# The last batch's attention tail in an order and banks of its own, filler rows issued by ScalarE, two steps of each batch moved by one q unit

## The chip, the cores and the metric
The kernel runs on one core of a Trainium2 chip. The metric is device time in microseconds (us) from start to end of one launch. Engines by short name: PE is TensorE (matmuls; PEld its weight loads), DVE is VectorE, ACT is ScalarE, POOL is GpSimd, SP the sync engine that issues most DMAs. SBUF is on-chip memory, PSUM holds the results of matmuls in eight banks of 128 partitions x 2 KB.

## The reference, cut to what matters
8 batches of 512 tokens, width 256, all in float32:

```python
h = conv31_depthwise(embed_table[x]) + conv_b
n = layernorm(h)
q, k, v = split(n @ w_qkv)                    # 16 heads of 64
q = softmax(q * 64**-0.5, over the 64 columns of a head)
k = softmax(k, over the 512 tokens)
h = h + ((k^T q per head) applied to v) @ w_out + b_out
n = layernorm(h)
p = sigmoid(n @ router_w.T); the two best of 8 experts, weights normalised
h = h + sum over those two: w * (relu(n @ W1[e])**2) @ W2[e]   # widths 4 x 256, 4 x 512
```

Since q is not mixed over tokens, each batch folds context, v and w_out into one 256 x 256 matrix m, so that the attention's output is n @ m.

## The kernel before
**Stages.** First the convolution, to about 93 us. Then `attend` works through the 8 batches, to about 487 us. Then `experts` goes through 71 tiles of 128 queue rows, each with the weights of one expert, to the end.

**How a batch of `attend` is cut.** Products in full float32 precision of the large ones are made from three float32r products (high x high, high x low, low x high: `split_product`), so most operands exist as a pair `_hi`, `_lo`: ACT copies the high part out of PSUM, DVE subtracts it to get the low part. For batch b: `xt` turns the normalised rows; `xt_high` and `xt_low` make their pair; eight `q_unit` (6 matmuls of 512 columns each) give q; for each, DVE takes the maximum and subtracts it (`q_shift`), ACT takes the exponential (`q_exps`), DVE sums (`q_total`), POOL normalises (`q_norm`). Eight `k_unit` give k turned, with `k_max` on DVE and `k_exp` on ACT, `k_turn` on PE (4 transposes into bank 3 or 4) and `k_take` on ACT out of it. `k_turn(b, c)` waits until `k_take` of c - 2 has emptied the bank.

**The tail of a batch** (12 uses of banks 5, 6, 7 in turn, `tail_bank`): `context_of` 0 and 1 (k^T q; DVE's `context_take` scales it), `g_of` 0 and 1 (context x w_out; ACT's `g_take` 0 to 3 empty the four banks), `m_of` (16 products in true float32), `m_high` and `m_low`, `attention_of` (24 products), `add_attention` and `ln2_stats` on DVE, `root2` on POOL (the reciprocal root), `ln2_apply` (the normalised rows, written to the tile `row`), `x2_turn`, `x2_take`, `router`, `logits_take`, `router_turn`, `prob_exp`, then on DVE `route_best` (the two best experts; ends in `counted`), `ranks` on PE (how many tokens go to each expert before this one) and `route_slots` on DVE (the queue slot of each row; ends in `slot`), last `enqueue` on POOL: 8 indirect DMAs of 128 rows of 258 floats each to `queue_d` in HBM.

**The order is written out by hand.** Every engine has a function `step(b, prev, nxt, old)`, called once per batch, in which the tail of `prev` and the routing of `old` are laced between the q and k work of b. `steps` calls it for n = -1 to 9, so the last two calls (b is None) hold only the tail of batch 7 and the routing of batches 6 and 7. In those calls stand also `w1_high` and `w1_low` (the expert weights w1 are split in high and low, in two pieces kk of 3072 columns) and `w1_pads` (POOL zeroes the padding). On SP, the last piece of w2 (`raw_in[3]`, 1536 KB) is loaded when `w1_low(0)` is done, after the store of batch 7's rows.

**Between the stages.** The engines' queues are in order. After `slot` of batch 7, DVE works out the table of tiles (`table.end_i`, `ends_ready`; at last `table.ready`). SP waits for `ends_ready` and writes one filler block of 128 rows after each of the 8 experts' queues: a register load (L764) and a DMA (L765) each. Then it waits until all fillers have landed (`table.filled`), reads the first 8 tile addresses into registers (`row_at`, L1546), waits for all enqueued rows (`queued`) and loads 8 tiles (L1551). ACT and DVE split w2 (`w2_high(2)`, `w2_high(3)`, `w2_low(2)`, `w2_low(3)`) before the first tile's `x_high` and `x_low`.

Of the kernel before, what the change touches and what calls it, by code (L numbers as in the profile page):

```python
# [20 lines left out]
F32 = mybir.dt.float32  # L21
# [90 lines left out]


class Dispatch:
# [3 lines left out]
    def __init__(self, sbuf, sem):  # L118
# [14 lines left out]
            "table_consts", "filler_ready", "ends_ready", "filled", "table_chain", "table_ready"))  # L133

# [27 lines left out]
def tower(nc, x, embeddings, conv_w, conv_b, w_qkv, w_out, b_out, router_w, w1, w2, out):  # L162
    top = ExitStack()
    with top:
# [35 lines left out]
        with ExitStack() as attn_ctx:  # L200
# [8 lines left out]
            with ExitStack() as ctx:  # L209
                attending = attend(nc, ctx, sem, bank, ident, base, base0, rw_t, w1, w2, h_d, store, h_in, loaded, h_stored, raw_in,  # L210
                       table, queue_d, out, second_half, wqk_hi, wqk_lo, wv_t, wo, bo_all,
                       w1_parts, w1_hi_ready, w1_lo_ready, w1_zero)
        with ExitStack() as ctx:
            expert_work = experts(nc, ctx, sem, bank, ident, store, raw_in, table, queue_d, out, w1_parts, w1_lo_ready,
                                  w1_zero, attending.queued, attending.stored)
# [401 lines left out]
def attend(nc, ctx, sem, bank, ident, base, base0, rw_t, w1, w2, h_d, store, h_in, loaded, h_stored, raw_in,  # L617
           table, queue_d, out, second_half, wqk_hi, wqk_lo, wv_t, wo, bo_all,
           w1_parts, w1_hi_ready, w1_lo_ready, w1_zero):
    def sbuf(name, shape, dt=F32):  # L620
# [49 lines left out]

    stored = [sem(f"stored{i}") for i in range(2)]
# [6 lines left out]
        sem(n) for n in ("q_shifted", "q_exp_ready", "q_inv_ready", "q_ready", "k_max_ready"))  # L678
    k_exp_ready, k_psum, k_ready, tail_chain, tail_psum = (
# [23 lines left out]

    def steps(engine, step):
# [10 lines left out]
        for n in range(-1, BATCHES + 2):  # L715
            step(at(n), at(n - 1), at(n + 1), at(n - 2))

    def sync(sp):
# [38 lines left out]
        steps(sp, step)  # L757

        sp.wait_ge(w1_lo_ready, 1)
        sp.dma_start(raw_place(store, 3), raw_piece((w1, w2), 3)).then_inc(raw_in[3], 16)  # L760

        sp.wait_ge(table.ends_ready, 1)
        for e in range(EXPERTS):
            at = sp.value_load(table.end_i[0:1, e:e + 1], min_val=0, max_val=FILLER_ROW)  # L764
            sp.dma_start(queue_d[bass.ds(at, P), :], table.filler[:]).then_inc(table.filled, 16)  # L765
    def gpsimd(pool):
# [68 lines left out]
        def enqueue(b):  # L835
            wait_apart(pool, slots_ready, b.nth(1, 1), pool_passed)
            for c in range(TOPK):
                for t in range(TT):
                    pool.indirect_dma_start(  # L839
                        out=queue_d, in_=row[:, t, c, :], in_offset=None,  # L840
# [14 lines left out]
        def step(b, prev, nxt, old):  # L855
            enqueue(old)
            if b is None:
                w1_pads(prev)
# [12 lines left out]
        steps(pool, step)  # L871

    def scalar(act):
# [63 lines left out]
        def step(b, prev, nxt, old):  # L937
# [12 lines left out]
            if b is None:  # L950

                w1_high(prev, 0)
                w1_high(prev, 1)
# [833 lines left out]
```

## Time and profile before

| | |
|---|---|
| median of 3 runs | 737.45 us (732.85 to 738.35) |
| the profiled execution | 736.28 us, its span 734.6 us |
| busy share of the span | PE 86%, PEld 75%, DVE 64%, ACT 42%, POOL 44% |
| batches 0 to 7 (93 to 450 us) | PE busy 340.31 of 357 us |
| last tail to first expert tile (450 to 510 us) | PE busy 21.11 of 60 us |
| experts (510 to 734 us) | PE busy 198.72 of 224 us |

Times in rows of the trace are us from the start of the span. In a timeline row: start, length, engine, line, operation, output <- inputs, how many; in brackets the idle time of the engine before it and what ended it. L877 is a helper's line for all copies of ACT, L1311 that of all split products of `attend`. A PE row's length holds the time for the last result to come out; so the next product can start before it ends. SPq and ACTq are DMA issues on those engines.

### The profile page before, as it was taken

Reading aid. Unit: us, or ns where it says so; the run is one execution under the profiler, and the core shown is the slowest. Engines: PE = TensorE matmul, PEld = TensorE weight load, DVE = VectorE, ACT = ScalarE, POOL = GpSimd, SP = SyncE. Lnnn points to the kernel's source line nnn. Section 1 sums busy time; section 2 is a strip of 40 time slices with the busy share of each in tenths; the row PEclk is TensorE's granted clock in tenths of the full one; section 3 lists DMA queues with packets and bytes.
Section 4 is the critical chain, followed back from the end, with each engine's and each line's share of the span. In section 5 each row is a group of like instructions: output and inputs, shape, how many; then the busy total and the mean of one; then the engine's idle time right before and its main releaser. Section 6 shows DMA issues by size and latency. Waiting matters only on the chain.

```text
span 734.6 us, 15772 instructions
## 1 busy us (share of the span) xinstructions
PE 632.1 (86%) x5032; PEld 547.8 (75%) x5032; DVE 469.7 (64%) x1216; ACT 306.8 (42%) x668; POOL 322.0 (44%) x292
## 2 busy tenths in 40 slices
PE   6997579999999999999999997523999999988881
PEld 6897457787877878778778785512899999987871
DVE  6475585777779777797787963573554554555540
ACT  3460135343353443533435335330544544555541
POOL 6350250330814608237073260635254454466574
PEclk9999689999999999999999999855999999999996
DMA  6551990010111101112010010423355445466663
GB/s 227 191 105 23 207 341 11 2 57 3 58 58 52 66 1 60 57 45 73 2 59 30 31 57 2 143 95 108 52 83 81 75 82 81 76 112 111 106 97 45
DMA packets 37216, 58.12 MB, mean 79 GB/s; under 512 B 5726, under 2 KB 31066, under 8 KB 36506
## 3 DMA queue, kind: packets, MB, share of 16 engines
q1 hardware_dynamic: 22434, 36.14, 16.9%
q0 software_dynamic: 14160, 20.13, 15.3%
q8 instruction: 61, 1.00, 0.6%
q10 hardware_dynamic: 520, 0.51, 0.2%
q14 instruction: 41, 0.34, 0.2%
HBM read 28.30 MB, written 27.42 MB: 76 GB/s over the span
## 4 chain that ended last, share of the span: by engine, by line
PE 65%; DVE 11%; DMA 7%; issue 5%; ACT 5%; POOL 3%; SPq 3%; DVEq 0%; POOLq 0%; ACTq 0%
PE bank L1311 20%; PE bank L1703 16%; PE bank L1383 8%; DMA out<-y,token_at 5%; PE bank L1354 4%; PE bank L1371 2%; PE bank L1719 2%; PE bank L521 2%; PE bank L522 2%; DVE xn L1009 2%; PE bank L542 2%; PE bank L1340 2%; POOL out L1583 2%; ACT k_exps L895 2%; DVE row L1089 1%
## 5 line engine op out<-in xcount | busy, mean ns | idle before, releaser
L1583 POOL DMA_INDIRECT out<-y,token_at x71 | 111.6, 1572 | 109.7 <-SPq L1563 107.6
L839 POOL DMA_INDIRECT queue_d<-row,slot x64 | 68.8, 1075 | 165.8 <-DVE slot L1148 148.7
L1660 DVE SCALAR_TENSOR_TENSOR act_w<-relu,queue_rows 128x512 f32<-128x512 f32 (+1 forms) x71 | 44.6, 629 | 102.5 <-ACT relu L1606 52.3
L1311 PE MATMUL bank<-xt_hi,w_first 128*128 128x512 f32 x256 | 95.1, 417 | 0.9 <-DVE second_half L1026 0.9
L1311 PE MATMUL bank<-w_first,xt_hi 128*128 128x512 f32 x256 | 83.8, 409 | 2.2 <-DVE xt_lo L1016 1.5
L831 POOL TENSOR_TENSOR second_half<-second_half,q_inv 128x512 f32<-128x512 f32 x64 | 64.9, 1041 | 44.0 <-DVE q_inv L1035 43.8
L887 ACT ACTIVATE second_half<-second_half 128x512 f32<-128x512 f32 x64 | 39.6, 632 | 87.9 <-DVE second_half L1026 87.9
L895 ACT ACTIVATE k_exps<-bank,k_negmax 128x512 f32<-128x512 f32 x64 | 44.1, 690 | 75.3 <-DVE k_negmax L1042 75.1
L1703 PE MATMUL bank<-w_hi,a_hi 128*128 x214 | 66.0, 308 | 1.6 <-DVE a_lo L1666 1.1
L1703 PE MATMUL bank<-w_lo,a_hi 128*128 x214 | 59.9, 280 | 0.1
L1606 ACT ACTIVATE relu<-bank 128x512 f32<-128x512 f32 (+1 forms) x71 | 35.4, 498 | 58.7 <-PE bank L1703 57.9
L1703 PE MATMUL bank<-w_hi,a_lo 128*128 x214 | 59.6, 278 | 0.0
L1311 PEld LDWEIGHTS bank<-w_first,xt_hi 128*128 128x128 f32 x256 | 46.9, 192 | 15.6 <-issue 2.7
L1383 PE MATMUL bank<-g,wv_t 128*128 128x256 f32 x256 | 56.7, 380 | 1.2 <-ACT g L877 1.2
L1311 PEld LDWEIGHTS bank<-xt_hi,w_first 128*128 128x128 f32 x256 | 49.2, 192 | 11.3 <-DVE second_half L1026 1.8
L1023 DVE TENSOR_REDUCE q_max<-bank 128x8 f32<-128x512 f32 x64 | 42.1, 657 | 22.6 <-PE bank L1311 22.6
L1383 PEld LDWEIGHTS bank<-g,wv_t 128*128 128x128 f32 x256 | 48.6, 190 | 8.4 <-ACT g L877 1.6
L1042 DVE TENSOR_REDUCE k_negmax<-bank 128x1 f32<-128x512 f32 x64 | 42.8, 680 | 13.4 <-PE bank L1311 13.1
L1311 PE MATMUL bank<-w_first,xt_lo 128*128 128x512 f32 x128 | 50.9, 398 | 0.0
L1311 PE MATMUL bank<-xt_lo,w_first 128*128 128x512 f32 x128 | 50.8, 397 | 0.0
L1703 PE MATMUL bank<-w_first,x_hi 128*128 x142 | 40.1, 364 | 9.7 <-DVE x_lo L1648 6.5
L1693 PE MATMUL bank<-ident,queue_rows 128*128 128x128 f32 x142 | 27.7, 279 | 23.3 <-DMA queue_rows<-queue_d 23.3
(183 smaller groups left out, 1564.3 us busy)
## 6 DMA issues: line engine op xcount, KB each, us to landing
queue_rows<-queue_d SPq DMA_DIRECT2D x71, 129.0 KB, 2.3
store<-in_L_ffn_w SPq DMA_DIRECT2D x4, 1536.0 KB, 9.2
out<-res SPq DMA_DIRECT2D x8, 512.0 KB, 2.9
h_d<-store SPq DMA_DIRECT2D x6, 512.0 KB, 9.0
h_in<-h_d SPq DMA_DIRECT2D x6, 512.0 KB, 4.0
windows<-taps_d SPq DMA_DIRECT2D x4, 512.0 KB, 5.8
wqk<-in_L_attn_w_qkv SPq DMA_DIRECT2D x1, 2048.0 KB, 13.9
out<-y,token_at POOLq DMA_INDIRECT x71, 4.0
```

What stands on the lines that cost most here:

```text
L831: nc.gpsimd.tensor_tensor(v, v, q_inv[:, b.par, u].unsqueeze(2).to_broadcast([P, 8, DH]), ALU.mult).then_inc(q_ready, 1)
L839: pool.indirect_dma_start(out=queue_d, in_=row[:, t, c, :], in_offset=None, out_offset=bass.IndirectOffsetOnAxis(ap=slot[:, TT * c + t:TT ...
L887: nc.scalar.activation(v, v, ACT.Exp, scale=SCALE).then_inc(q_exp_ready, 1)
L895: nc.scalar.activation(k_exps[:, c % 2], qk_bank(10 + c)[:], ACT.Exp, bias=k_negmax[:, c:c + 1], accum_out=k_sum[:, b.par, c:c + 1]).then_ ...
L1023: link(nc.vector.tensor_reduce(q_max[:, u % 2], src, AX, ALU.max), q_chain, b, Q_LINKS, 2 * u + 1 - (u > 0))
L1042: nc.vector.tensor_reduce(k_negmax[:, c:c + 1], qk_bank(10 + c)[:], AX, ALU.max, negate=True).then_inc(k_max_ready, 1)
L1311: last = nc.tensor.matmul(o, a, c, start=(n == 1), stop=(n == 3 * len(pairs)))
L1383: last = nc.tensor.matmul(tail_bank(6)[:, DIM * kk:DIM * kk + DIM], wv_t[:, a, P * kk:P * kk + P], g[:, a], start=(a == 0), stop=(a == PAI ...
L1583: pool.indirect_dma_start(out=out, in_=y[:, j % RING, :], in_offset=None, compute_op=ALU.add, out_offset=bass.IndirectOffsetOnAxis(ap=toke ...
L1606: nc.scalar.activation(relu[:, u % 2, 0:width], bank[2 + u % 2][:, 0:width], ACT.Relu).then_inc(relu_ready, 1)
L1660: nc.vector.scalar_tensor_tensor(out=act_w[:, u % 2, 0:width], in0=relu[:, u % 2, 0:width], scalar=rows[:, u, DIM:DIM + 1], in1=relu[:, u ...
L1703: last = nc.tensor.matmul(o, a, c, start=(n == 1), stop=(n == parts))
```

## The change
1. In each batch, `k_turn(b, 7)` on PE goes from the end of the batch to behind `q_unit(b + 1, 0)`; `g_of(prev, 1)` goes behind `q_unit(b, 5)`; ACT takes `q_exps(b, 3)` between `g_take` 1 and 2.
2. The last two calls of `step` are replaced by an order of their own for batch 7's tail. It uses banks 0 to 6, which q and k no longer need, in place of the three tail banks, and its rows go to `row_last`, a piece of the tile `k`. `context_of(7, 1)` follows `context_of(7, 0)` at once; `m_of_last` starts on the first four heads' pairs and writes its halves to two banks; high, low and product of m go half by half (`m_high_of`, `m_low_of`, `attention_of_last`); `normalize_last` does DVE's sums and statistics by halves; `route_slots` of batch 7 takes the steps that need no ranks ahead of the wait for them, and adds to `base` after `slot`.
3. The splitting of w1 goes piece by piece between these. POOL zeroes pads first, then issues six of batch 6's eight enqueues, then `root2(7)`, then the other two. SP loads the last piece of w2 before it stores batch 7's rows. `w2_high(3)` goes on ACT ahead of `x2_take(7, 0)`, `w2_low(3)` on DVE ahead of `route_best(7)`, `w2_low(2)` behind the first two `x_low`.
4. The 8 filler blocks are issued by ACT, after `w2_high(2)` and before `x_high(0)`; SP reads its first 8 addresses before it waits for the fillers.

```diff
@@ scalar (attend), last batch
-        steps(act, step)
+        last, ahead = steps(act, step)
+        prob_exp(ahead)
+        w1_high(last, 0)
+        g_take(last, 0)
+        g_take(last, 1)
+        g_take(last, 2)
+        g_take(last, 3)
+        w1_high(last, 1)
+        m_high_of(last, 0)
+        m_high_of(last, 1)
+        w2_split.high(act, 3)
+        x2_take(last, 0)
+        x2_take(last, 1)
+        logits_take(last)
+        prob_exp(last)
@@ vector (attend), last batch
-        steps(dve, step)
+        last, ahead = steps(dve, step)
+        narrow, wide = 0, 1
+        route_best(ahead)
+        context_take(last, 0)
+        w1_low(0, narrow)
+        context_take(last, 1)
+        w1_low(0, wide).then_inc(w1_lo_ready, 1)
+        route_slots(ahead)
+        w1_low(1, wide)
+        m_low_of(last, 0)
+        w1_low(1, narrow).then_inc(w1_lo_ready, 1)
+        m_low_of(last, 1)
+        normalize_last(last)
+        ln2_apply(last)
+        w2_split.low(dve, 3, 1)
+        route_best(last)
+        route_slots(last)
@@ tensor (attend)
         def step(b, prev, nxt, old):
             q_unit(b, 0)
+            k_turn(prev, 7)
             router_turn(old)
...
             q_unit(b, 4)
             g_of(prev, 0)
+            q_unit(b, 5)
             g_of(prev, 1)
-            q_unit(b, 5)
             q_unit(b, 6)
...
             k_turn(b, 6)
-            k_turn(b, 7)
-
-        steps(pe, step)
+
+        last, ahead = steps(pe, step)
+        k_turn(last, 7)
+        router_turn(ahead)
+        context_of(last, 0)
+        context_of(last, 1)
+        g_of(last, 0)
+        ranks(ahead)
+        g_of(last, 1)
+        m_of_last(last)
+        attention_of_last(last)
+        x2_turn(last)
+        router(last)
+        router_turn(last)
+        ranks(last)
@@ gpsimd (attend), last batch
-        steps(pool, step)
+        last, ahead = steps(pool, step)
+        w1_pads(last)
+        enqueue(ahead, 0, 6)
+        root2(last)
+        enqueue(ahead, 6)
+        enqueue(last)
@@ sync (attend) and scalar (experts)
         sp.wait_ge(w1_lo_ready, 1)
         sp.dma_start(raw_place(store, 3), raw_piece((w1, w2), 3)).then_inc(raw_in[3], 16)
-
-        sp.wait_ge(table.ends_ready, 1)
-        for e in range(EXPERTS):
-            at = sp.value_load(table.end_i[0:1, e:e + 1], min_val=0, max_val=FILLER_ROW)
-            sp.dma_start(queue_d[bass.ds(at, P), :], table.filler[:]).then_inc(table.filled, 16)
+        store_h2(last)
...
         attention_left(act)
-        w2_high(2)
-        w2_high(3)
+        w2_split.high(act, 2)
+
+        act.wait_ge(table.ends_ready, 1)
+        for e in range(EXPERTS):
+            at = act.value_load(table.end_i[0:1, e:e + 1], min_val=0, max_val=FILLER_ROW)
+            act.dma_start(queue_d[bass.ds(at, P), :], table.filler[:]).then_inc(table.filled, 16)
         x_high(0, 0)
         x_high(1, 1)
@@ sync (experts)
         sp.wait_ge(table.ready, 1)
-        sp.wait_ge(table.filled, 16 * (EXPERTS + 3))
         attention_left(sp)
...
         first_rows = [row_at(j) for j in range(SLOTS)]
+        sp.wait_ge(table.filled, 16 * (EXPERTS + 3))
         sp.wait_ge(queued, 16 * TOPK * TT * BATCHES)
@@ vector (experts)
         attention_left(dve)
-        w2_low(2)
-        w2_low(3)
         x_low(0, 0)
         x_low(1, 1)
+        w2_split.low(dve, 2, 2)
@@ vector, the new order of route_slots for the last batch
+            if b.is_last():
+                gates()
             dve.wait_ge(rank_psum, b.nth(1, 1))
...
+            if not b.is_last():
+                next_base()
+                gates()
```

## Rows read from the trace of the kernel before
**Rows 1.** Waits of PE, 112 to 456 us: who waited <- for whom: total, times, longest

```profile
PE bank L1371 <- ACT g L877: 6.4, 7, 0.9
PE bank L1340 <- ACT k L877: 4.0, 8, 1.1
```

**Rows 2.** Timeline of PE: last turn of k, first q unit, first k unit

```profile
401.54 0.63 PE L1340 MATMUL bank<-ident,k_exps 128*128 128x128 f32 x4 [0.39 <-ACT k L877]
401.93 0.70 PE L1311 MATMUL bank<-w_first,xt_hi 128*128 128x512 f32 x2
...
421.03 0.40 PE L1311 MATMUL bank<-xt_hi,w_first 128*128 128x512 f32 x1
```

**Rows 3.** Timeline of DVE in the same batch: xt_low, q_total(3), q_shift(5)

```profile
399.79 1.29 DVE L1016 TENSOR_TENSOR xt_lo<-bank,xt_hi 128x512 fp32r<-128x512 f32 x2 [0.64 <-ACT xt_hi L877]
...
418.57 0.69 DVE L1033 TENSOR_REDUCE q_sum<-second_half 128x8 f32<-128x512 f32 x1 [0.33 <-ACT second_half L887]
...
420.08 0.69 DVE L1026 TENSOR_TENSOR second_half<-bank,q_max 128x512 f32<-128x512 f32 x1
```

**Rows 4.** Timeline of PE, batch 7's tail: context_of 0 and 1, g_of 0

```profile
448.62 2.08 PE L1354 MATMUL bank<-second_half,k 128*64 128x64 f32 x64 [0.62 <-issue]
...
451.90 2.09 PE L1354 MATMUL bank<-second_half,k 128*64 128x64 f32 x64
454.86 1.09 PE L1371 MATMUL bank<-wo,context 64*64 64x256 f32 x16 [0.87 <-issue]
```

**Rows 5.** Chain that ended last, batch 7's tail: start, length, what

```profile
459.15 7.19 PE bank L1383 x32
...
467.78 3.11 PE bank L1311 x24
```

**Rows 6.** Timeline of ACT and DVE: w1_high(0), w1_low(0)

```profile
458.98 2.86 ACT L934 ACTIVATE w_first<-store 128x1024 fp32r<-128x1024 f32 x2
...
461.87 3.43 DVE L1156 TENSOR_TENSOR w_first<-store,w_first 128x1024 fp32r<-128x1024 f32 x2 [5.21 <-ACT w_first L934]
```

**Rows 7.** Transfer of the last piece of w2: KB, us from issue to landing

```profile
store<-in_L_ffn_w SPq DMA_DIRECT2D x1, 1536.0 KB, 8.1
```

**Rows 8.** Timeline of DVE: place and slot of batch 7, then w2_low

```profile
485.21 0.19 DVE L1132 TENSOR_TENSOR place<-bank,base 128x32 f32<-128x32 f32 x1 [0.63 <-PE bank L1436]
...
487.33 0.17 DVE L1148 CAST slot<-slotf 128x8 uint32<-128x8 f32 x1
...
494.55 6.70 DVE L1643 TENSOR_TENSOR w_lo<-store,w_hi 128x2048 fp32r<-128x2048 f32 x3
```

**Rows 9.** Timeline of POOL: enqueues of batch 6 (first row) and of batch 7

```profile
464.23 1.90 POOL L839 DMA_INDIRECT queue_d<-row,slot  x1 [0.30 <-issue]
...
488.33 1.10 POOL L839 DMA_INDIRECT queue_d<-row,slot  x1 [13.20 <-DVE slot L1148]
...
495.12 2.55 POOL L839 DMA_INDIRECT queue_d<-row,slot  x1 [0.30 <-issue]
497.98 4.10 POOL L839 DMA_INDIRECT queue_d<-row,slot  x1 [0.30 <-issue]
502.38 0.96 POOL L839 DMA_INDIRECT queue_d<-row,slot  x1 [0.30 <-issue]
```

**Rows 10.** Timeline of SP: the 8 filler DMAs, first issue to last

```profile
489.42 9.32 SPq L765 DMA_DIRECT2D queue_d<-filler  x8
```

**Rows 11.** Chain that ended last, between the stages

```profile
498.41 2.58 DMA queue_d<-filler
501.05 0.28 SPq L1546
...
505.84 2.11 DMA queue_rows<-queue_d
```

**Rows 12.** Timeline of ACT at the kernel's start: a DMA that ACT issues

```profile
0.82 0.48 ACTq L370 DMA_DIRECT2D store<-in_L_tok_embed_table  x1
```

**Rows 13.** Issues by line, 503 to 507 us: the last enqueue, us from issue to landing

```profile
queue_d<-row,slot POOLq DMA_INDIRECT x1, 2.5
```

More of the change, by code:

```diff
@@ L713, in at @@
             return batches[n] if 0 <= n < BATCHES else None
-        for n in range(-1, BATCHES + 2):
+        for n in range(-1, BATCHES):
             step(at(n), at(n - 1), at(n + 1), at(n - 2))
+        return batches[-1], batches[-2]
     def sync(sp):
@@ L755, in step @@
             store_h2(prev)
[L757 removed]
+        last, _ = steps(sp, step)
         sp.wait_ge(w1_lo_ready, 1)
         sp.dma_start(raw_place(store, 3), raw_piece((w1, w2), 3)).then_inc(raw_in[3], 16)
[L762 to L765 removed]
+        store_h2(last)
     def gpsimd(pool):
@@ L1147, in route_slots, with w1_low @@
             then(nc.vector.tensor_reduce(slotf[:], placed[:], AX, ALU.add))
+            if b.is_last():
+                dve.wait_ge(queued, b.nth(16 * TOPK * TT, 0))
             nc.vector.tensor_copy(slot[:], slotf[:]).then_inc(slots_ready, 1)
+            if b.is_last():
+                next_base()
             assert n[0] == ROUTE_LINKS, n[0]
-        @unless_none
-        def w1_low(last, kk):
+        def w1_low(kk, part):
             dve.wait_ge(w1_hi_ready, kk + 1)
-            hi, lo = (piece(store, kk, w1_parts[kk][:, part]) for part in range(2))
-            for (src, high), (_, dst) in zip(hi, lo):
-                done = nc.vector.tensor_tensor(dst, src, high.bitcast(F32), ALU.subtract)
-            done.then_inc(w1_lo_ready, 1)
+            hi, lo = (piece(store, kk, w1_parts[kk][:, n])[part] for n in range(2))
+            return nc.vector.tensor_tensor(lo[1], hi[0], hi[1].bitcast(F32), ALU.subtract)
         def step(b, prev, nxt, old):
@@ L1590, in scalar @@
     def scalar(act):
-        def w2_high(n):
-            act.wait_ge(raw_in[n], 16)
-            for src, dst in piece(store, n, w2_hi):
-                last = nc.scalar.activation(dst, src, ACT.Copy)
-            last.then_inc(w2_hi_ready, 1)
         def x_high(j, u):
@@ L1639, in vector @@
     def vector(dve):
-        def w2_low(n):
-            dve.wait_ge(w2_hi_ready, n - 1)
-            for (src, hi), (_, dst) in zip(piece(store, n, w2_hi), piece(store, n, w2_lo)):
-                last = nc.vector.tensor_tensor(dst, src, hi.bitcast(F32), ALU.subtract)
-            last.then_inc(w2_lo_ready, 1)
         def x_low(j, u):
```

205 lines of the change are left out of this document (146 added, 59 removed).

## The prediction
> **What bounds the kernel now.** I read four views. First the busy time by stretch (the table above): in the batches and in the experts PE is busy nearly all the time, but from 450 to 510 us only 21 of 60 us. So there are two places to gain: what little PE waits for inside a batch, and the chain from batch 7's last k unit to the first expert tile, in which the engines work one after another.
>
> Second, PE's waits over the batches [rows 1]. Only two are left that come back in each batch. `g_of(1)` waits 0.9 us, seven times, 6.4 us in all, until ACT has emptied the tail bank that `g_of(0)` has just filled. `k_turn(7)` waits until `k_take(5)` is through, 0.4 us in most batches.
>
> Third, the timeline of the tail, which shows what each product of PE waited for. `context_of(7, 1)` begins at 451.90 though `context_of(7, 0)` is out at 450.7: the ranks of batch 6 stand between them in PE's queue and wait for DVE [rows 4]. `g_of(0)` then waits for a bank that DVE reads in `route_slots(6)`; `g_of(1)` waits for ACT as in each batch; `m_of` starts at 459.15 and the attention's product at 467.78, 1.43 us after m is finished, because high and low part must be made between [rows 5].
>
> Fourth, the chain that ended last between the stages [rows 11]. After `slot` (487.33 + 0.17 = 487.50, rows 8) it goes through SP: eight fillers from 489.42 to 498.41, landed at 501.0, then the eight address reads, then the load at 505.84 [rows 10, 11]. From `slot` to that load it is 18.34 us. POOL's chain beside it is hardly shorter: the last enqueue starts at 502.38 and lands 2.5 us later, 504.9 [rows 9, 13]. Both must shrink for a gain.
>
> **Part 1, inside the batches.**
> *g_of(1).* A q unit of 1.4 us put between covers the 0.9 us in which ACT empties the bank. The q unit needs nothing that is late: the moved unit 5 wants the bank of unit 2, whose shift is long done. Seven batches: **6.4 us** [rows 1].
>
> *k_turn(7).* Before, PE waits 0.39 us for it, turns (401.54 to 401.93, 0.39 us of PE), and starts q unit 0 at 401.93 [rows 2]. After, q unit 0 may start as soon as `xt_low` is out: 399.79 + 1.29 = 401.08, say 401.13 with the signal [rows 3]. That is 0.80 earlier, and the turn now comes behind it: 0.80 - 0.39 = 0.41 us. Seven changes of batch: **2.9 us**. The cost is a new wait, on `xt_low` in place of `k_take`; it is counted here, since without it the whole 0.39 and more would come back. `k_take(7)` comes later by about 1 us, and the first reader of k is three q units away, some 3 us.
>
> *Is DVE next?* DVE does about 23 us of work on q without a pause, and k unit 0 needs the bank that `q_shift(5)` reads: ready at 420.08 + 0.69 = 420.77, used at 421.03, slack 0.26 [rows 2, 3]. PE would arrive 0.91 + 0.41 = 1.3 us earlier, at 419.7. DVE starts 0.8 earlier, with q unit 0, and loses the 0.33 us wait on ACT's exponential, as `q_exps(3)` goes ahead of `g_take(2)` [rows 3]: 420.77 - 1.1 = 419.65. Just even; I book no loss, and 0 to 0.4 us in each of seven batches (0 to 3 us) for the range.
>
> **Part 2, batch 7's tail, on the old clock.** `context_of(1)` follows at once: 450.7 to 452.7. `g_of(0)` needs no tail bank: 452.75; the ranks 0.45; `g_of(1)` to 455.25 (each about 1.05, rows 4). So `m_of` starts 3.9 us earlier than 459.15 and its 7.19 us end at 462.45. Its first half (kk = 0) is complete 1.8 us before that. By then ACT has split w1's second piece (free of `g_take` at 456.4, plus 2.86 = 459.3) and DVE has done the wide part of the low one (2/3 of 3.43 = 2.29, until 461.6) and the low part of m's half, 462.05 [rows 6]. So the product starts right at 462.5, and the 1.43 us between m and it are gone. Ends: 470.9 before, 465.6 after, **5.3 us**. The halves in `normalize_last` bring nothing: the last half waits for the same product, and DVE has 3.6 us to do from 464.85 on, which ends where the old order (2.7 us from the product's end) would.
>
> What is moved beside it: POOL. `root2(7)` is now queued behind pads and six enqueues. These begin at `slot` of batch 6, which is 1.5 us later than before (`w1_low(0)` stands ahead of it on DVE), about 458.95, and take 6 x 1.27 plus what the w1 work on DVE stretches. In the trace the enqueue that met `w1_low(0)` took 1.90 instead of 0.96 [rows 9]; with 1.2 us in all POOL is free at 467.6, and the statistics come at 468.3. Slack 0.7: even. The w2 piece: SP issues it at 456.2, lands 8.1 later [rows 7], 464.3; ACT splits it in 2.75 us; `x2_take` wants ACT at 472.7. Hidden, with 5 us to spare. `w2_low(3)`, half of the 6.70 us [rows 8], lies where DVE waits for the turned rows, the router and its turn, nearly 5 us: hidden.
>
> **Part 3, routing of batch 7.** DVE idles 0.63 us for the ranks [rows 8], now filled with steps that stood behind, and the 0.2 us for `base` goes behind `slot`: **0.8 us**.
>
> **Part 4, slot to first load.** Fillers: `ends_ready` comes 0.2 later after `slot` (base). Before, first issue 1.92 after `slot`, last 8.99 after that (7 steps of 1.28), landing 2.58 [rows 8, 10, 11]: 13.5 on SP. On ACT there is no row of such a loop. Bounds: SP's pace of 1.28 us per filler, and 0.15 to 0.3 us more each, since a plain DMA issue took ACT 0.48 at the start [rows 12] where SP's took 0.33 (498.41 + 0.33 is the end of the 9.32, rows 10). I take 0.12 more each, near SP: 13.5 + 0.2 + 0.8 = 14.5 us; ends of the range 13.3 and 16. POOL: first enqueue 0.83 after `slot`, then 1.10 + 0.30, six times 0.96 + 0.30, 0.3 for what the table's work on DVE stretches, landing 2.5: 12.6 us [rows 9, 13], if the two long ones (2.55 and 4.10, rows 9) are normal again. They coincide with `w2_low` on DVE (494.55 to 501.25, rows 8), which is moved away. The six before them had fillers in flight too, and were not long. SP's address reads: table ready 7.1 + 0.2 after `slot` (`w2_low` starts behind the table at 494.55, rows 8), plus 4.8 for the reads (501.05 to 505.84, rows 11), 12.1: not the last. So load at 14.6 in place of 18.34: **3.7 us**.
>
> [...]
>
> `w2_low(2)` now runs behind `x_low(1)`, 3.35 us until 513.4; the first `square` began at 513.38. Hidden, 0 to 0.3 us. The experts are otherwise untouched.
>
> **Sum.** 6.4 + 2.9 + 5.3 + 0.8 + 3.7 = 19.1 us. The profiled execution took 736.28, so 717.2; it lay 1.2 under the median, so **718.4 us**, 2.6% less.
>
> **Rivals.**
> *DVE bounds the q phase.* For it: slack 0.26 only, and even by my own working. Against: it starts earlier by the same step. Price 0 to 0.4 a batch, then 721; if nothing at all came back in the batches, 727.7. Chance 0.12.
> *The long enqueues stay*, because fillers in flight caused them. Then POOL's chain takes 17.4 (504.9 - 487.5) and part 4 gives 0.9: 721.2. Against: enqueues 2 to 6. Chance 0.1.
> *POOL is late for root2.* If DVE's w1 work stretches the six enqueues by as much as the 4.7 us that `w2_low` cost two of them (2.55 + 4.10 - 2 x 0.96, rows 9), POOL is free at 471.1, 2.8 after the statistics: 721.2. Chance 0.1.
> *ACT's fillers are slow*, each 0.5 more than I take: +4: 722.4. Chance 0.08.
> *Other side: slower than before.* ACT stands on the path between the stages, `x_high(0)` behind its eight fillers. If a register load with a dependent DMA costs ACT far more than SP, it eats all. The others give 15.4, so it must bring the load to 18.3 + 15.4 = 33.7 us after `slot`: 3.8 us per filler, three times SP's 1.28. Nothing in the rows shows that; two such together with no gain in the batches would need only 2.7. Chance 0.02.
> *The change moves little*, gains in the tail lost to something that I don't see: 730 to 736. Chance 0.03.
> Forecast as worked out, within 3 us: 0.5; better than that, as waits behind the removed ones go too: 0.05.
>
> **How the numbers follow.** The range takes the forecast with 3 us below, the bounds of ACT's pace, and all single rivals but the batches' full loss: 713 to 725, where I leave 0.13 outside. For this kernel about 1% (730.1) can be told from no change. All cases but the last two and a piling up of several lie below it: faster 0.94, same 0.04, slower 0.02.
>
> **What would show it.** Right: no wait of `g_of` on ACT; `q_unit` 0 waits under 0.1 us for `xt_low`; the period of a batch falls by 1.3 us; `m_of` starts within 8 us after `context_of(7, 0)` begins (10.5 before), product directly behind it; no enqueue of batch 7 over 1.3 us; 14.6 us from `slot` to the first load. Wrong: k unit 0 waits for DVE; `rstd` over 1.6 us after its statistics; the fillers more than 1.6 us apart.

## The result and the profile after

| | before | changed |
|---|---|---|
| median | 735.15 us (4 runs, 732.22 to 738.35) | 715.25 us (4 runs, 714.01 to 718.2) |
| ratio | | 0.9723, 95% interval 0.9673 to 0.9773 |
| profiled execution | 736.28 us, span 734.6 | 714.98 us, span 713.3 |

Forecast was 718.4 us in 713 to 725. The two spans cut at the same events show where the time went (from the timelines; "turn of k" is `k_turn`'s first transpose, "slot" the end of the last write to `slot`, "load" the issue of the first `queue_rows` load):

| stretch | before | changed | gain | forecast |
|---|---|---|---|---|
| start to first turn of k | 105.59 | 104.91 | 0.68 | 0 |
| first to last turn of k | 341.67 | 333.03 | 8.64 | 9.3 |
| last turn of k to slot | 40.24 | 34.00 | 6.24 | 5.3 + 0.8 |
| slot to load | 18.34 | 13.99 | 4.35 | 3.7 |
| load to end | 228.76 | 227.37 | 1.39 | 0 |

The first and the last row hold nothing that the change touches, apart from `w2_low(2)` at the start of the experts. In the profiles of the twelve runs below they vary by themselves: load to end lay between 227.2 and 229.6 us, whether the tail was old or new. The first turn of k came at 105 us in these two profiles, at 103 to 104 in `low_back`, `fill_act_before`, `fill_sp_after` and `enq_first`, which were measured together, and at 114 to 116 in the others. (So times are compared only with those of the kernel before that were measured beside them; between groups, stretches are compared. What shifts the start is not known: two groups that bear the same chip number gave 103 to 104 and 116.) The three rows in the middle gain 19.2 us, forecast 19.1.

**Inside the batches.** PE's waits, 93 to 470 us of the changed kernel, that answer to [rows 1]; L1427 is the split product, L1456 the turn of k, L1556 `x2_turn`:

```profile
PE bank L1556 <- DVE k L1184: 6.5, 1, 6.5
PE bank L1456 <- ACT k_exps L945: 3.4, 1, 3.4
PE bank L1427 <- DVE second_half L1091: 1.6, 4, 0.5
PE bank L1427 <- DVE xt_lo L1081: 0.7, 1, 0.7
...
PE bank L1456 <- ACT k L927: 0.6, 1, 0.6
```

The seven waits of `g_of` on ACT are gone, and of the eight on `k_take` only the last batch's is left. None comes back per batch. Timeline of PE at a change of batch (last turn but one, q unit 0, last turn, routing's turn, unit 1), then the two halves of g with unit 5 between, and k unit 0:

```profile
392.28 0.66 PE L1456 MATMUL bank<-ident,k_exps 128*128 128x128 f32 x4
392.96 0.70 PE L1427 MATMUL bank<-w_first,xt_hi 128*128 128x512 f32 x2
...
394.42 0.60 PE L1456 MATMUL bank<-ident,k_exps 128*128 128x128 f32 x4
394.85 0.27 PE L1576 MATMUL bank<-ident,x_t 128*128 128x128 f32 x1
394.88 0.71 PE L1427 MATMUL bank<-w_first,xt_hi 128*128 128x512 f32 x2
...
405.25 1.09 PE L1488 MATMUL bank<-wo,context 64*64 64x256 f32 x16
406.27 0.73 PE L1427 MATMUL bank<-w_first,xt_hi 128*128 128x512 f32 x2
...
407.85 1.09 PE L1488 MATMUL bank<-wo,context 64*64 64x256 f32 x16
...
411.73 0.39 PE L1427 MATMUL bank<-xt_hi,w_first 128*128 128x512 f32 x1
```

DVE beside it: `xt_low`, and the second half of `q_shift(5)`, which frees the bank for the k unit at 411.73:

```profile
391.57 1.29 DVE L1081 TENSOR_TENSOR xt_lo<-bank,xt_hi 128x512 fp32r<-128x512 f32 x2 [0.51 <-ACT xt_hi L927]
...
410.68 0.69 DVE L1091 TENSOR_TENSOR second_half<-bank,q_max 128x512 f32<-128x512 f32 x1
```

`xt_low` ends at 392.86 and q unit 0 starts at 392.96. `q_shift(5)` ends at 411.37, 0.36 us before it is needed.

**Batch 7's tail.** Timeline (all engines): the two contexts as one row, `g_of(0)`, `m_of_last`, `w1_high(1)`, the last wide `w1_low`, `m_low_of(0)`, the product's first row:

```profile
439.31 4.27 PE L1470 MATMUL bank<-second_half,k 128*64 128x64 f32 x128 [0.62 <-issue]
443.51 1.09 PE L1488 MATMUL bank<-wo,context 64*64 64x256 f32 x16
445.99 7.17 PE L1511 MATMUL bank<-g,wv_t 128*128 128x256 f32 x32
447.10 2.86 ACT L989 ACTIVATE w_second<-store 128x1024 fp32r<-128x1024 f32 x2
449.99 2.29 DVE L1261 TENSOR_TENSOR w_second<-store,w_second 128x2048 fp32r<-128x2048 f32 x1 [1.15 <-ACT w_second L989]
452.20 0.42 DVE L1133 TENSOR_TENSOR m_lo<-bank,m_hi 128x256 fp32r<-128x256 f32 x1
452.82 0.47 PE L1530 MATMUL bank<-m_hi,xt_hi 128*128 128x256 f32 x1
```

From the last turn of k to `m_of` it is 8.05 us (11.89 before), and the product starts where `m_of` ends, even 0.3 us ahead of its last result, in place of 1.43 us behind it [rows 5]. In five other profiles with the new tail the two contexts took 3.95 us in place of 4.27 and this stretch was 7.73; the cause of the longer contexts here is open.

**Slot to load.** Timeline of POOL: last of the first six enqueues, `root2`, one of the two that follow it, then three of batch 7's, the last one among them:

```profile
457.42 0.96 POOL L886 DMA_INDIRECT queue_d<-row,slot  x1 [0.30 <-issue]
459.14 0.23 POOL L861 TENSOR_SCALAR var_eps<-mean_var 128x4 f32<-128x4 f32 x1 [0.76 <-DVE mean_var L1174]
...
462.41 4.13 POOL L886 DMA_INDIRECT queue_d<-row,slot  x1 [0.30 <-issue]
...
474.02 1.35 POOL L886 DMA_INDIRECT queue_d<-k,slot  x1 [0.30 <-issue]
475.68 1.25 POOL L886 DMA_INDIRECT queue_d<-k,slot  x1 [0.31 <-issue]
...
482.29 0.96 POOL L886 DMA_INDIRECT queue_d<-k,slot  x1 [0.30 <-issue]
```

Timeline of ACT's queue, the fillers:

```profile
473.97 8.44 ACTq L1796 DMA_DIRECT2D queue_d<-filler  x8
```

Timeline of SP's queue, the loads:

```profile
485.93 9.01 SPq L1715 DMA_DIRECT2D queue_rows<-queue_d  x9
```

None of batch 7's enqueues takes 2.55 or 4.10 us any more [rows 9]. ACT is through with the fillers at 482.4, 10.5 us after `slot`, faster than I took (its steps are 1.16 us, SP's 1.28, rows 10). The chain that ended last (start, us, what) shows what the load waits for now, the last enqueue's landing:

```profile
482.29 3.41 DMA queue_d<-k,slot
...
485.93 2.07 DMA queue_rows<-queue_d
```

So POOL's chain ends last here, and in `after_again` and `enq_first`. A third chain is close behind it: in `tail_only` and `old_exps` the same view names SP's address reads. They begin 7.3 us after `slot` and end 13.2 and 13.1 us after it, with the load at 13.48 and 13.38.

### The profile page after: what moved, and what is told of

Read it like the earlier page. It is cut to its first block, busy times and chain, and to the rows that moved or that the text cites. A ratio compares the mean times of both kernels' runs of the same rounds, so it can differ in the third digit from the quotient of the medians.

```text
span 713.3 us, 15773 instructions
## 1 busy us (share of the span) xinstructions
PE 631.3 (89%) x5032; PEld 546.0 (77%) x5032; DVE 468.4 (66%) x1219; ACT 306.8 (43%) x669; POOL 321.1 (45%) x292
## 4 chain that ended last, share of the span: by engine, by line
PE 77%; DMA 8%; DVE 6%; issue 3%; POOL 2%; ACT 1%; SPq 1%; DVEq 0%; ACTq 0%; POOLq 0%
PE bank L1427 26%; PE bank L1859 16%; PE bank L1500 7%; DMA out<-y,token_at 7%; PE bank L1470 5%; PE bank L1456 4%; PE bank L1875 2%; PE bank L1488 2%; PE bank L546 2%; PE bank L547 2%; PE bank L567 2%; PE bank L1849 2%; PE bank L529 1%; PE bank L1418 1%; PE bank L1556 1%
## 5 line engine op out<-in xcount | busy, mean ns | idle before, releaser
L886 POOL DMA_INDIRECT queue_d<-row,slot x56 | 59.7, 1066 | 129.0 <-DVE slot L1253 114.2
L1427 PE MATMUL bank<-xt_hi,w_first 128*128 128x512 f32 x256 | 94.8, 416 | 0.9 <-DVE second_half L1091 0.9
L1427 PE MATMUL bank<-w_first,xt_hi 128*128 128x512 f32 x256 | 84.7, 412 | 3.1 <-DVE xt_lo L1081 2.3
L1427 PEld LDWEIGHTS bank<-w_first,xt_hi 128*128 128x128 f32 x256 | 46.2, 192 | 19.6 <-issue 6.8
L1427 PEld LDWEIGHTS bank<-xt_hi,w_first 128*128 128x128 f32 x256 | 49.2, 192 | 11.0 <-DVE second_half L1091 1.8
L1107 DVE TENSOR_REDUCE k_negmax<-bank 128x1 f32<-128x512 f32 x64 | 42.8, 679 | 14.8 <-PE bank L1427 13.8
L1427 PE MATMUL bank<-w_first,xt_lo 128*128 128x512 f32 x128 | 50.8, 397 | 0.0
L1427 PE MATMUL bank<-xt_lo,w_first 128*128 128x512 f32 x128 | 50.7, 396 | 0.0
L1500 PE MATMUL bank<-g,wv_t 128*128 128x256 f32 x224 | 49.5, 379 | 0.0
L1777 ACT ACTIVATE y<-bank 128x256 f32<-128x256 f32 x71 | 27.4, 385 | 46.1 <-PE bank L1859 29.1
L1500 PEld LDWEIGHTS bank<-g,wv_t 128*128 128x128 f32 x224 | 42.5, 190 | 6.0
```

Source lines behind the costliest of these rows:

```text
L886: pool.indirect_dma_start(out=queue_d, in_=row_of(b)[:, t, c, :], in_offset=None, out_offset=bass.IndirectOffsetOnAxis(ap=slot[:, TT * c + ...
L1107: nc.vector.tensor_reduce(k_negmax[:, c:c + 1], qk_bank(10 + c)[:], AX, ALU.max, negate=True).then_inc(k_max_ready, 1)
L1427: last = nc.tensor.matmul(o, a, c, start=(n == 1), stop=(n == 3 * len(pairs)))
L1500: last = nc.tensor.matmul(tail_bank(6)[:, DIM * kk:DIM * kk + DIM], wv_t[:, a, P * kk:P * kk + P], g[:, a], start=(a == 0), stop=(a == PAI ...
```

## The experiments

### The parts of the loop alone: loop_only and tail_only

`loop_only` is the kernel before with the three moves inside the batches:

```diff
             q_unit(b, 0)
+            k_turn(prev, 7)
...
             g_of(prev, 0)
+            q_unit(b, 5)
             g_of(prev, 1)
-            q_unit(b, 5)
...
-            k_turn(b, 7)
...
             g_take(prev, 1)
+            q_exps(b, 3)
             g_take(prev, 2)
             g_take(prev, 3)
-            q_exps(b, 3)
```

> The kernel before with only the moves inside the batches (last turn of k, second half of g, the third exponential). If the parts add up, m_of's period falls from 46.66 to 45.41 us as in the changed kernel, and the time by 8.7 us, to about 726.5 (ratio 0.988). Rival: the old tail takes back part of it, since its waits start from DVE's side: then the period falls but the time from the last turn of k to the first load grows above 58.6 us (505.84 - 447.26).

`tail_only` is the changed kernel with the same lines put back.

> The changed kernel with the old order inside the batches: last turn of k at the batch's end, g's halves side by side, old order of the exponential. If the parts add up, the period is 46.66 us again, the span from the last turn of k to the first load stays at 48.0 us (485.93 - 437.94), and the time is 8.7 us above the changed kernel, about 724.5. Rival: the new tail profits from the new order of the batches; then that span grows above 48.5 us.

Measured, on one chip: `loop_only` 737.01 us against 744.64, ratio 0.9908 (0.9882 to 0.9933); `tail_only` 733.05 us, ratio 0.9866 (0.9832 to 0.99). The product of the two ratios is 0.9775; the changed kernel itself gave 0.9723 and, in `after_again` below, 0.9736. So the parts add up within the intervals. `loop_only` gained less than the 0.988 that I expected. Neither rival came: from the last turn of k to the load it was 58.0 us in `loop_only` (above 58.6 was the rival's sign) and 47.2 us in `tail_only` (above 48.5). By stretches of the profiles, each period and each of the two stretches behind it the median of the batches:

| kernel | period of m_of | xt to context_of | g_of to m_of | last turn of k to slot |
|---|---|---|---|---|
| before | 46.66 | 8.10 | 8.65 | 40.24 |
| kturn_only | 46.36 | 7.77 | 8.65 | 40.26 |
| loop_only | 45.55 | 7.77 | 7.85 | 40.24 |
| tail_only | 46.56 | 7.98 | 8.65 | 33.67 |
| changed | 45.41 | 7.63 | 7.85 | 34.00 |

The table showed two things that I had not expected. The loop alone comes to 45.55 us, not 45.41. And `tail_only`, which leaves PE's order in the batches as it was, still has a period 0.1 us shorter than before, all of it between `xt` and `context_of`. (Readings of a stretch differ by 0.02 us between batches; one batch of each profile has a period about 0.3 us longer.)

### The last turn of k alone: kturn_only

```diff
             q_unit(b, 0)
+            k_turn(prev, 7)
             router_turn(old)
...
-            k_turn(b, 7)
```

> The kernel before with only the last turn of k behind the next batch's first q unit. My prediction gave it 0.41 us per batch with a new end: PE then waits for xt_low in place of k_take. Period of m_of 46.2 us (46.66 - 0.45), from x2_turn to the next g_of 19.15 in place of 19.6 us, and 8.6 us from g_of to m_of as before. Rival: the two moves share a gain, and alone this one gives less than 0.3 or more than 0.6 us.

741.56 us in the one run. The gain is in the right stretch, 0.33 us per batch (8.10 to 7.77 in the table), not 0.41 to 0.45. The move of g, with that of the exponential, then takes 0.80 more off another stretch: the two share nothing.

### The 0.12 us that neither move explains: stats_only

DVE's rows of `tail_only` and of the kernel before differ in one place of each batch. In the kernel before, the first statistic began behind the end of the second sum; in `tail_only`, before that end. Timeline of DVE, the kernel before, second sum and statistics:

```profile
387.53 0.69 DVE L1069 TENSOR_TENSOR res<-bank,res 128x512 f32<-128x512 f32 x1 [0.68 <-PE bank L1311]
388.25 1.40 DVE L1076 BATCH_NORM_STATS2 stats<-res 128x6 f32<-128x256 f32 x4
```

The same in `tail_only`:

```profile
394.19 0.69 DVE L1143 TENSOR_TENSOR res<-bank,res 128x512 f32<-128x512 f32 x1 [0.68 <-PE bank L1427]
394.79 1.39 DVE L1149 BATCH_NORM_STATS2 stats<-res 128x6 f32<-128x256 f32 x4
```

The change had split `add_attention` and `ln2_stats` into halves to reuse them for batch 7, and with that the wait of the first two statistics became one for the first half of the sum, in every batch. `stats_only` does that in the kernel before:

```diff
-            dve.wait_ge(res_added, b.nth(2, 2))
             for t in range(TT):
+                if t % 2 == 0:
+                    dve.wait_ge(res_added, b.nth(2, t // 2 + 1))
                 last = nc.vector.bn_stats(stats2[:, t], res[:, b.par, t])
```

> The kernel before with one thing of the change that my prediction passed over: in every batch the first two statistics wait only for the first half of the sum, so DVE need not drain the second sum before them. The trace of the changed kernel and of the one with the new tail only show 0.12 us per batch less between xt and context_of than their k and g moves explain. If this is the cause, the period falls from 46.66 to 46.54 us. If the cause is elsewhere (addresses, semaphores), it stays at 46.66.

Measured: period 46.56, xt to context_of 7.98 us, as in `tail_only`. That settles it: this wait is worth the 0.12 us. PE gets them back in `xt`: its eight transposes make a row of 1.28 to 1.30 us in the kernel before, `kturn_only` and `loop_only`, and of 1.16 to 1.17 in `stats_only`, `tail_only` and the changed kernel. The sum of the loop is 0.80 (g) + 0.33 (k) + 0.12 (statistics) = 1.25 us per batch, the whole of 46.66 - 45.41. (Its single time, 746.04 against a median of 744.34, tells nothing: its last tail met a spell of low clock, see below.)

### Is DVE the next bound? old_exps

```diff
             g_take(prev, 1)
-            q_exps(b, 3)
             g_take(prev, 2)
             g_take(prev, 3)
+            q_exps(b, 3)
```

(in the changed kernel)

> The changed kernel with the third exponential on ACT behind all four g_take again, all else kept. My claim that DVE is level with PE at k unit 0 predicts a loss: g_take 3 now ends near 410.0 on the changed kernel's clock, the exponential at 410.6, q_total(3) starts at 410.65 in place of 409.17, q_shift(5) ends 1.5 us later at 412.9 and k unit 0 waits for it from 411.73: period 46.6 us in place of 45.41, the move of g's second half is worth nothing. Rival: DVE has room, the period stays at 45.4 us.

Measured: period 47.12 us in place of 45.41, slower than the kernel before with its 46.66; 736.93 us against 744.64, one run. Timeline of DVE: `q_total(3)` waits 1.80 us for the exponential.

```profile
430.40 0.69 DVE L1098 TENSOR_REDUCE q_sum<-second_half 128x8 f32<-128x512 f32 x1 [1.80 <-ACT second_half L937]
...
431.92 0.69 DVE L1091 TENSOR_TENSOR second_half<-bank,q_max 128x512 f32<-128x512 f32 x1
```

Timeline of PE: a product of the k units waits 1.44 us for its bank and starts 0.05 us behind the end of the last shift of q on DVE (431.92 + 0.69).

```profile
432.66 0.50 PE L1427 MATMUL bank<-xt_hi,w_first 128*128 128x512 f32 x1 [1.44 <-issue]
```

So in the new order of PE the third, seemingly cosmetic move of one ACT instruction is worth 1.7 us per batch, more than the two moves on PE together. It confirms that DVE follows PE closely here: 1.80 us of delay on DVE, less the slack of 0.36, is the 1.44 that PE waits. I had expected a loss of 1.2 us and it is 1.7; the 0.3 us beyond PE's wait I did not trace.

### POOL and root2: enq_first

```diff
-        enqueue(ahead, 0, 6)
-        root2(last)
-        enqueue(ahead, 6)
+        enqueue(ahead)
+        root2(last)
```

> The changed kernel with all eight enqueues of batch 6 ahead of root2 of batch 7. In the changed kernel POOL is free at 458.38 and starts root2 at 459.14, so my claim that POOL is nearly level predicts that two enqueues more, 2 x 1.26 us, put root2 1.8 to 2.0 us later, and slot and the end with it (717 us). Rival: POOL overlaps or the statistics come later anyway, and slot stays where it is, 34.0 us after the last turn of k.

Measured: last turn of k to slot 35.49 us; without the edit it is 33.67 to 34.00. POOL's rows: the eighth enqueue, then at once the root, which waits for nothing.

```profile
458.47 0.96 POOL L886 DMA_INDIRECT queue_d<-row,slot  x1 [0.30 <-issue]
459.45 0.25 POOL L861 TENSOR_SCALAR var_eps<-mean_var 128x4 f32<-128x4 f32 x1
```

1.5 to 1.8 us lost, a little less than the 1.8 to 2.0 that I expected. Six enqueues leave 0.6 us in the changed kernel; that a seventh, at 1.26 us, would be too much is worked out from this and was not run. The time was 716.98 us in the one run, against 733.89 for the kernel before and no run of the changed kernel beside it.

### Slot to load: low_back, fill_act_before, fill_sp_after

These three were run once each, beside one run of the kernel before with 733.89 us: `low_back` took 713.69 us, `fill_act_before` 734.38, `fill_sp_after` 715.92. Single times tell little (the first is below the changed kernel's median, the second had a spell of low clock, see below), so the stretches are read. `low_back` (changed kernel):

```diff
+        w2_split.low(dve, 2, 2)
         x_low(0, 0)
         x_low(1, 1)
-        w2_split.low(dve, 2, 2)
```

> The changed kernel with w2_low(2), 3.4 us of DVE with two SBUF inputs, ahead of the first two x_low again, so that it runs right after the table of tiles, while POOL still issues batch 7's enqueues. If DVE's work stretches them, the enqueues that start about 6.6 to 10 us after slot take up to 4 us in place of 0.96, and the first load comes 1.5 to 3 us later than the 14.0 us after slot of the changed kernel. If the fillers in flight caused the long ones, all enqueues stay below 1.4 us and the load stays at 14.0.

Timeline of POOL, one of batch 7's enqueues:

```profile
476.77 2.54 POOL L886 DMA_INDIRECT queue_d<-k,slot  x1 [0.31 <-issue]
```

Timeline of DVE, `w2_low(2)`:

```profile
476.18 3.43 DVE L156 TENSOR_TENSOR w_lo<-store,w_hi 128x2048 fp32r<-128x2048 f32 x2
```

The one enqueue inside DVE's 3.43 us took 2.54 us and ended 0.3 us before it did; the others stayed under 1.4, though ACT's fillers were in flight with all of them. That is the cause of the long enqueues, and the rival (fillers in flight) is out. The row of `w2_low(2)` holds two instructions, of 2.29 and 1.2 us. The enqueue ended 0.84 us after the first of them. The same holds in all 14 profiles: each of batch 6's and 7's enqueues that a `tensor_tensor` with both inputs in SBUF stretched ended 0.83 to 0.84 us after that instruction, whether it was one of `w1_low` or `w2_low` or one of 0.75 us on the table. In the kernel before these are the enqueues of 1.24, 1.90, 1.25, 2.55 and 4.10 us. The load came at 14.60 us after slot. The same stretch without `w2_low` there was 13.38 to 13.99, so the cost is 0.6 to 1.2 us, less than the 1.5 to 3 expected: one enqueue was caught, not two, and though the last was issued 1.6 us later than in the changed kernel, it landed 2.43 us after that, not 3.41.

`fill_act_before` is the kernel before with part 4 alone: the loop of fillers moved from SP to ACT behind `w2_high(3)`, the wait for them behind `first_rows`.

> The kernel before with only the fillers issued by ACT and the addresses read ahead of the wait for them; w2_low stays where it was, beside the enqueues. If two chains run beside each other, POOL's end at 17.4 us after slot now decides and the load comes at 17.5 to 18.0 in place of 18.34: gain below 1 us. If SP's chain was the only one that counted, the load comes at 14 to 14.5.

Slot to load 17.61 us in place of 18.34: 0.7 gained, or less, since in `kturn_only`, `loop_only` and `stats_only`, which leave this part as it was, it was 17.78 to 17.88. POOL's rows still hold 2.55 and 4.10 us, its last enqueue starts 14.9 us after slot and lands 2.49 later. So the fillers on ACT bring next to nothing while `w2_low` lies beside the enqueues. `w2_low` moved away by itself, with all else as before, was not run.

`fill_sp_after` is the changed kernel with the fillers on SP again (behind `store_h2(last)`), the wait still behind `first_rows`.

> The changed kernel with the fillers issued by SP again, ahead of its address reads; the wait for the fillers stays behind the reads. SP: ready to read at 11.1 us after slot (0.2 + 1.92 + 9.0), eight reads of 0.55 us to 15.5, load at 15.6 in place of 14.0 us: 1.6 us later. If POOL's chain alone counts, it stays at 14.0; if the order of the wait and not the engine brought the gain, also.

15.48 us, 1.5 us more than the changed kernel, as expected: SP has to do fillers and address reads one after the other. It is also 2.3 to 2.9 us less than before, so `w2_low` moved away and the reads ahead of the wait bring the larger part, and the engine of the fillers the rest. Its steps here were 1.18 us, not 1.28.

### A second profile of the changed kernel: after_again

> The changed kernel itself, unchanged, as the measure for the first of these runs on the same chip: from the last turn of k to slot 34.0 us, from slot to the first load 13.4 to 14.0, period 45.4 us.

725.99 us against 744.34, ratio 0.9736 (0.9702 to 0.977); period 45.41, last turn of k to slot 33.67, slot to load 13.58 us, all as expected or 0.3 us less.

### Can PE's clock be held? warm and warm2

In the changed kernel PE's clock is low between the stages. Windows of the changed kernel: us, then busy us of PE, PEld, DVE, ACT, POOL, then the granted clock, DMA share, GB/s:

```profile
458.00:459.00 1.00, 0.00 (x0) 0.00 (x0) 0.79 (x6) 0.00 (x0) 0.38 (x1) 1.00 0.59 234
459.00:460.00 1.00, 0.00 (x0) 0.00 (x0) 0.00 (x0) 0.00 (x0) 0.78 (x2) 0.53 0.98 365
...
492.00:493.00 1.00, 1.00 (x5) 0.70 (x4) 1.00 (x2) 0.01 (x1) 0.00 (x0) 0.50 0.00 0
493.00:494.00 1.00, 1.00 (x6) 0.87 (x5) 0.96 (x2) 0.87 (x2) 0.00 (x0) 0.90 0.00 0
```

PE ends its product at 456.0 and stands idle; the clock falls from 1.00 (2.4 GHz) to 0.50 (1.2 GHz) at 459, and comes back at 493, some 5 us after the first transposes of the experts at 488.05. `warm` fills the waits:

```diff
+        def warm(n):
+            for _ in range(n):
+                nc.tensor.transpose(bank[7][:, 0:P], ident[:], ident[:])
...
         attention_of_last(last)
+        warm(50)
         x2_turn(last)
         router(last)
         router_turn(last)
+        warm(20)
         ranks(last)
+        warm(148)
```

> The changed kernel with 218 transposes of the identity into bank 7, which nobody reads, in PE's three long waits of batch 7's tail: 50 ahead of x2_turn, 20 ahead of the last ranks, 148 ahead of the first expert tile. In the changed kernel the granted clock is 0.50 from about 459 to 493.5 us. If idle PE is what lowers it and these hold it at 1.0, x2_turn takes 1.0 us in place of 1.97, the router 0.65 in place of 1.1, its turn 0.27 in place of 0.48, and about 2 us come back in the first tiles: 3.5 us in all, 711.7 us, provided 0.11 us each lets them end before the waits do. Rival: such filling does not count, the clock stays at 0.50, each takes 0.23 us and the last block ends 17 us late: 735 us or more.

724.01 us, ratio 0.9711 (0.9684 to 0.9738), on the same chip as `after_again` with 0.9736 (0.9702 to 0.977): 2 us in the medians, but the intervals overlap. Timeline of PE:

```profile
465.73 5.08 PE L1630 MATMUL bank<-ident 128*128 128x128 f32 x45
471.81 1.09 PE L1556 MATMUL bank<-ident,k 128*128 128x128 f32 x8 [1.01 <-DVE k L1184]
...
489.38 0.31 PE L1630 MATMUL bank<-ident 128*128 128x128 f32 x1 [0.31 <-issue]
490.77 0.38 PE L1630 MATMUL bank<-ident 128*128 128x128 f32 x2 [1.08 <-issue]
492.21 6.75 PE L1630 MATMUL bank<-ident 128*128 128x128 f32 x48 [1.06 <-issue]
498.80 0.60 PE L1856 MATMUL bank<-ident,queue_rows 128*128 128x128 f32 x4
```

The filling counts for the clock: it was granted 1.00 from 459 to 489, where the changed kernel had 0.50. `x2_turn` takes 1.09 us in place of 1.97, the router 0.65 in place of 1.1, its turn 0.33 in place of 0.48, and last turn of k to slot is 32.27 us, 1.4 less than `after_again`. But behind 489 PE issues nothing for 0.3 to 1.1 us at a time though no transpose waits for anything, the clock falls behind these pauses (0.62 from 491 to 493), and the block ends at 499.0, after the rows (load at 494.20 and about 2.1 us to land). So of the 3.5 us expected only those before slot came. `warm2` shortens the block to 112 and moves `w2_low(2)` between POOL's first memset and `x_low(0)`.

> The kernel with the 218 transposes, corrected by its trace: the last block ended at 499.0 us though the first rows had landed at 496.3, and w2_low(2) on DVE kept the first square until 503.7. Now 112 in place of 148 in the last block, and w2_low(2) goes between POOL's last enqueue and the first x_low (it waits for the first of POOL's two memsets). If both readings are right, the first expert transpose follows the landing of the rows by less than 0.3 us (2.5 us gained), the wait of act_turn on act_w goes (0.75 us), and the ratio to the kernel before falls from 0.971 to 0.967. Rival: the pauses of 1.1 us in which PE issued nothing come back and let the clock fall, then only part of it, 0.970.

724.4 us, ratio 0.9703 (0.9679 to 0.9727): no gain over `warm` that can be told, and the 0.967 expected was missed, though both readings were right: the first expert transpose starts at 497.12, about 0.1 us behind the landing (load at 494.95, some 2.1 us to land), and PE no longer waits for the first `act_w`. What came is the rival. The pauses came back (0.4 to 0.96 us each between 489 and 493), the clock was 0.61 and 0.54 in the two windows from 490 to 498, last turn of k to slot was 32.71 us, 0.4 more than in `warm`, and the load came at 14.74 us after slot, later than in the changed kernel. Neither version is shown to beat the changed kernel.

## Why the prediction was right, and where its terms were off

The mechanisms held: both waits of PE are gone from the batches, the tail's product follows m without a gap, and the load comes earlier because several chains were shortened together. That the three middle stretches come to 19.2 us where 19.1 were forecast is in part luck. The two moves in the batches brought 1.4 us less than forecast, an effect that I had not seen brought 0.8, and slot to load brought 0.65 more. One of the signs for "right" failed narrowly: an enqueue of batch 7 took 1.35 us, and I had said none over 1.3.

**g_of(1), 6.4 us forecast, 5.6 measured** (0.80 in each of seven batches). Mechanism right: the wait is gone and nothing took its place. The term was mis-sized. Starts of the kernel before show it: the two halves stood 2.01 us apart before and need 1.02, so 0.98 were lost, more than the 0.9 shown as idle; but the q unit between them now takes 1.58 us from start to start (406.27 to 407.85) where a q unit among q units takes 1.37. A q unit behind g takes 1.49 and one ahead of g 1.45 in the kernel before. So the two changes more between the kinds of product, out of g and back into it, cost 0.2 together.

**k_turn(7), 2.9 forecast, 2.3 measured** (0.33 each). The reasoning by `xt_low` holds; q unit 0 follows its end by 0.10 us, not 0.05. The rest, about 0.03 us, I can't place.

**Statistics, not forecast, 0.8 us** (0.12 each): the one step that my prediction missed. I read the new helpers as the old code in two pieces and did not see that a wait in the loop had become weaker. It shows in a diff only if each wait's value is compared, not its text.

**DVE level with PE: right, by a margin.** Forecast: the bank free at 419.65 for a need at 419.7. Measured slack 0.36 us, and `old_exps` shows what happens without it. The rival "DVE bounds the q phase" did not come.

**The tail, 5.3 forecast, 5.5 measured** from the last turn of k to the end of the attention's product (23.62 to 18.09). This part was run only as a whole, in `tail_only`; which of its steps brings what is read from the timelines. `m_of` starts 3.8 us earlier (3.9 forecast). The product starts 0.3 us before m's last result instead of with it, which I had not seen. From the product's end to slot it is 0.7 us less, where 0.8 was forecast for the routing.

**POOL nearly level, slack 0.7 forecast, 0.6 measured** (458.38 to 458.95); `enq_first` shows its price. The rival "POOL late" did not come, though two of the six enqueues were stretched, and the 4.13 us enqueue behind `root2` met `w2_low(3)` as expected where nobody waits.

**Slot to load, 3.7 forecast, 4.35 measured. Nearly the right sum, wrong last chain.** I had the fillers last, at 14.5, and POOL at 12.6. ACT was faster than SP (last filler issued 10.5 us after slot, where I had 11.9), and POOL slower than I took: the enqueues were stretched by 0.7 us in all by the table's work on DVE (I took 0.3), and the last landed 3.41 us after its issue, not 2.5. So POOL's chain, 13.8, ends last. The two errors went against each other. A third term was also too short: I had the address reads done at 12.1, with 4.8 us for the eight. They took 5.9 and 5.8 in `tail_only` and `old_exps` and ended last there, at 13.2 and 13.1. So two of the chains end within 1 us of each other, and shortening POOL's alone could bring no more than that.

**Port.** The Trainium skill (SBUF — State Buffer, "Who interferes with whom") says that a DVE instruction with two SBUF inputs contends with a GpSimd instruction that reads SBUF, because its second input comes through the read interface that they share. The traces fit that: 2.54 us in `low_back` for the enqueue caught, 0.96 for its neighbours, and the end always 0.83 to 0.84 us behind DVE's. The same section counts `tensor_tensor` among the operations that were not seen to stall a DMA. For these indirect enqueues the measurement decides otherwise: 4.13 us beside a `tensor_tensor` of 3.35.

**w2_low(2) hidden: right.** The first `square` starts 5.57 us after the first expert transpose, 5.38 before: 0.2 us, within the 0 to 0.3.

**Medians.** The forecast added 1.2 us since the profiled execution of before lay under its median. With a fourth run that median is 735.15, 1.1 under the profiled one. So 718.4 and 715.25 differ by 3.1, of which 2.3 is the median of before; the rest is the first and last stretch (2.1 us in the profile) less what the medians give back. The change has no part in those that the rows show.

## What to carry to other kernels

Count a term from starts, not from the idle time shown, and charge each change between kinds of product. Where several chains run to one wait, shorten them together, and after that ask which comes last: here the fillers on ACT alone gave 0.7 us at most, all edits together 4.35, and SP's chain and POOL's now end within 1 us of each other. When an order is moved on one engine, walk the ones that answer it: here the ACT instruction that was moved along decided over 1.7 us per batch.

## What the runs showed of the hardware

- An indirect enqueue of POOL that is caught by a DVE `tensor_tensor` with both inputs in SBUF ends 0.83 to 0.84 us after it, in all 14 profiles. So what a change will do to it can be estimated: it takes from its start to DVE's end, plus 0.84, in place of 0.96. (An enqueue of 1.42 us stood beside the `tensor_scalar` of `ln2_apply`; its cause was not tested.)

- The tail can meet a low clock that the average hides. In `fill_act_before`, whose tail is that of the kernel before, `m_of` took 8.88 us in place of 7.19: its granted clock was 0.59 and 0.50 from 456.3 to 460, after the gaps of PE between the contexts and g. (The kernel before has the same gaps, and its clock was 1.00 from 456 to 460; so what makes the difference is open.) `stats_only`, with the same tail, shows it too: `m_of` took 8.77 us (from 467.14), the granted clock was 0.62 from 466 to 470, and from the last turn of k to slot it was 41.7 us, against 40.24 to 40.26 in three other kernels with this tail. In none of the seven profiles with the new tail and no added work was that stretch over 34.0 us, apart from `enq_first`, where the enqueues explain it. Windows of `fill_act_before`, columns as above:

```profile
456.30:458.00 1.70, 1.66 (x5) 1.31 (x6) 0.00 (x0) 1.70 (x2) 1.39 (x2) 0.59 0.42 155
458.00:460.00 2.00, 2.00 (x6) 1.64 (x5) 0.94 (x1) 2.00 (x3) 1.39 (x3) 0.50 0.19 66
460.00:462.00 2.00, 2.00 (x10) 1.75 (x10) 2.00 (x2) 1.78 (x1) 1.70 (x2) 1.00 0.35 126
```

- A long run of PE instructions that wait for nothing stopped for 0.3 to 1.1 us at a time, from 488.6 on in both kernels with added transposes. The DMA engines were 33 to 63% busy in the windows with these pauses, but 66% from 485 to 489 in `warm`, where PE did not stop. What holds the instructions back was not tested.
- Of the fillers, DMAs with an address from a register, ACT issued one every 1.13 to 1.16 us, SP one every 1.28 in the kernel before and every 1.18 in `fill_sp_after`. So the step depends on more than the engine.
